# Four small matmuls of a pair of tiles on four quarters of the array instead of two

## The reference, cut to what matters

```python
W = weights[condition]                        # (64, 64, 64), one matrix per sequence
y = jnp.einsum('bct,bcd->bdt', x, W)          # mix over the channels
w = (unpacked - zero_point) * scale           # (1024, 1024), 6-bit values, scale and zero by output row
return x + jnp.einsum('bsk,nk->bsn', y, w) + bias
```

## Time and profile before

| | us |
|---|---|
| median of 3 runs | 293.28 (293.01 to 293.81) |
| the profiled execution's own time | 293.79 |
| its span, first to last instruction | 292.0 |
| TensorE matmuls busy | 285.5 (98%) |
| VectorE busy | 188.3 (65%) |
| GpSimd busy | 91.9 (31%) |
| ScalarE busy | 84.5 (29%) |
| granted TensorE clock | 1.00 of full speed |

### The profile page before, as it was taken

The page is one execution under the profiler, slowest core; times in us unless marked ns, Lnnn a source line. Parts: engine busy times, 40 slices in busy tenths (PEclk is TensorE's granted clock), DMA queues, the critical chain, the costliest instruction groups (busy, mean ns, idle before and its releaser), DMA issues.

```text
span 292.0 us, 8492 instructions
## 1 busy us (share of the span) xinstructions
PE 285.5 (98%) x3299; PEld 234.3 (80%) x3299; DVE 188.3 (65%) x255; ACT 84.5 (29%) x195; POOL 91.9 (31%) x39
## 2 busy tenths in 40 slices
PE   7999999999999999999999999999999999999995
PEld 3867888888888888888888888888888888888884
DVE  3687998655667565566756566675656667565554
ACT  3755334512406050240605023060602306030000
POOL 1019814314143432414343240434324043430000
PEclk9999999999999999999999999999999999999999
DMA  7983646442524344142524415143441510122112
GB/s 248 314 321 96 210 177 200 142 152 77 159 110 135 125 144 151 73 153 108 164 97 144 153 72 189 72 149 112 146 151 72 188 72 36 72 74 74 72 72 73
DMA packets 20547, 39.02 MB, mean 134 GB/s; under 512 B 6835, under 2 KB 7091, under 8 KB 20532
## 3 DMA queue, kind: packets, MB, share of 16 engines
q1 hardware_dynamic: 20100, 37.63, 37.2%
q10 hardware_dynamic: 432, 1.18, 1.1%
HBM read 22.02 MB, written 16.78 MB: 133 GB/s over the span
## 4 chain that ended last, share of the span: by engine, by line
PE 93%; DMA 2%; SPq 2%; ACT 1%; issue 1%; DVE 1%
PE o_ps L301 80%; PE y_ps L259 10%; DMA q_raw<-in_L_ffn_qweight_dram 2%; PE ysum_ps L318 1%; SPq L153 1%; SPq L149 1%; ACT qT L460 1%; PE y_ps L301 1%; DMA ids<-in_itok_B_dram 0%; PE ysum_ps L273 0%; PE qt_ps L283 0%; PE ysum_ps L347 0%; ACT junk L426 0%; SPq L138 0%; DVE q_int L520 0%
## 5 line engine op out<-in xcount | busy, mean ns | idle before, releaser
L301 PE MATMUL o_ps<-qT,y_hi 128*128 128x512 f32 (+1 forms) x520 | 200.6, 389 | 0.4 <-ACT qT L460 0.4
L301 PE MATMUL o_ps<-qT,y_lo 128*128 128x512 f32 (+1 forms) x520 | 198.1, 384 | 0.5 <-issue 0.5
L654 POOL TENSOR_TENSOR resid<-x_sb,bias_bc 128x1024 f32<-128x1024 f32 x32 | 90.8, 2840 | 168.1 <-DVE o_sb L558 149.3
L301 PEld LDWEIGHTS o_ps<-qT,y_hi 128*128 128x128 f32 x520 | 97.2, 188 | 21.9 <-issue 1.5
L301 PEld LDWEIGHTS o_ps<-qT,y_lo 128*128 128x128 f32 x520 | 97.2, 188 | 18.8
L550 DVE TENSOR_TENSOR o_sb<-o_ps,scale_bc 128x512 f32<-128x512 f32 x63 | 43.6, 692 | 82.2 <-PE o_ps L301 82.1
L435 ACT ACTIVATE y_hi<-y_ps 128x512 fp32r<-128x512 f32 x64 | 33.4, 602 | 161.2 <-PE y_ps L259 161.1
L558 DVE TENSOR_TENSOR o_sb<-o_sb,resid 128x512 f32<-128x512 f32 x63 | 52.6, 836 | 2.2
L530 DVE TENSOR_TENSOR y_lo<-y_ps,y_hi 128x512 fp32r<-128x512 f32 x64 | 40.0, 683 | 9.0 <-ACT y_hi L435 9.0
L539 DVE SCALAR_TENSOR_TENSOR resid<-zs_bc,ysum,resid 128x1024 f32<-128x1024 f32 x32 | 43.2, 1350 | 0.0
L259 PE MATMUL y_ps<-w_sb,x_sb 64*64 64x64 f32 x2048 | 35.2, 220 | 0.1
(11 more groups left out here) (33 smaller groups left out, 49.2 us busy)
## 6 DMA issues: line engine op xcount, KB each, us to landing
x_sb<-in_x_dram SPq DMA_DIRECT2D x32, 512.0 KB, 3.5
out_dram<-o_sb SPq DMA_DIRECT2D x63, 256.0 KB, 2.0
q_raw<-in_L_ffn_qweight_dram SPq DMA_DIRECT2D x5, 384.0 KB, 5.8
q_raw<-in_L_ffn_qweight_dram ACTq DMA_DIRECT2D x3, 384.0 KB, 5.1
w_sb<-in_L_cond_weights_dram SPq DMA_DIRECT2D x64, 16.0 KB, 2.0
bias_bc<-in_L_ffn_bias_dram SPq DMA_DIRECT2D x1, 512.0 KB, 8.7
zs_bc<-n_weight_zero_point_dram SPq DMA_DIRECT2D x1, 512.0 KB, 9.4
out_dram<-o_sb SPq DMA_DIRECT2D x2, 128.0 KB, 2.0
```

The costliest lines, as they stand in the source:

```text
L301: last = nc.tensor.matmul(bank, part[:, slot, kt, :], qT[:, kt, col:col + width], start=(kt == 0 and part is y_hi), stop=(kt == KT - 1 and ...
L654: nc.gpsimd.tensor_tensor(resid[:, j % RING, :], x_sb[:, j % RING, :], bias_bc[:], ALU.add).then_inc(xbias_ready, 1)
```

## The change

Only the second tile of a pair (odd `j`) is treated otherwise. Its `half` 0 still reads the upper row half, but writes partitions 64 to 127 of `ysum_ps`; its `half` 1 reads the lower row half and writes partitions 0 to 63 of `qt_ps`. These are the two quarters that the first tile's sums do not use. ScalarE reads the sums from these partitions and writes them to the same partitions of `ysum` as before, so for odd tiles its copy goes from one half of the partitions to the other. The number, the kind and the order of instructions are the same on every engine, and so are the semaphores; no bank of PSUM is used that was not used before.

```diff
                 for half in range(2):
                     rows = slice(half * C, (half + 1) * C)
-                    last = nc.tensor.matmul(ysum_banks[half][rows, slot:slot + 1], w_sb[rows, slot, rows],
+                    place = slice((half + j) % 2 * S, ((half + j) % 2 + 1) * S)
+                    last = nc.tensor.matmul(ysum_banks[half][place, slot:slot + 1], w_sb[rows, slot, rows],
                                             xsum[rows, slot:slot + 1], start=True, stop=True)
                     last.then_inc(ysum_ps_ready, 1)
...
                     act.wait_ge(ysum_ps_ready, t * 2 + half + 1)
-                    last = nc.scalar.activation(ysum[rows, slot:slot + 1], ysum_banks[half][rows, slot:slot + 1],
+                    place = slice((half + j) % 2 * S, ((half + j) % 2 + 1) * S)
+                    last = nc.scalar.activation(ysum[rows, slot:slot + 1], ysum_banks[half][place, slot:slot + 1],
                                                 ACT.Copy, scale=-1.0)
```

## The result

The changed kernel takes 291.63 us in the median of 11 runs (290.94 to 293.34), the kernel before 292.95 us in 11 runs (292.62 to 296.29). The ratio is 0.9942, with a 95% interval of 0.992 to 0.9964: faster by 0.6%, between 1.1 and 2.3 us. The ratio is not that of the two medians, which would be 0.9955 (1.32 us); both lie in the interval. The forecast was 291.9 us.

The account below looks back on a forecast made before the run. TensorE was taken as the bound, its sums-and-mix stage as long as the fullest array quarter. 13 steps x 0.105 us, about 1.4 us, off 293.28 gave 291.9 us; range 291.3 to 292.5, widened to 293.1 for rivals.

Parts of the forecast that it names:

- TensorE alone is the bound, and only the stage of sums and mix changes: Loop step: all 16.98 us are TensorE's; the 14.73 us linear layer stays, the effect lies in the other 2.25 us.
- The fullest quarter sets the stage, 36 loads against 34 at 0.058 us: Sums and mix: two weight loads fewer on each of the two fuller array quarters, 0.116 us less per step.
- The stagger: Head of the sums: third and fourth quarters start 0.01 to 0.02 us later, leaving about 0.10 us gain.
- 0.105 us per step, 1.4 us in all: Sums and mix: net gain per step, ends 0.05 and 0.13 us, taken over 13 steps.
- The median: Whole kernel: 293.28 us, the median of the runs before, less 1.4 us gives 291.9 us.
- Ahead of 52.9 us nothing changes: Start-up before the loop: unchanged, so 0 us in the total.
- The sum: Whole kernel: 1.4 us off gives a span of 290.6 us and a profiled execution of 292.4 us.
- ScalarE's crossing copies cost nothing: ScalarE's four copies per step, two crossing partition halves: 0 us, with some 13 us of cover if dearer.
- Rival A: Sums: second tile's loads start 0.055 us late on a shared row half; gain 0.06 us per step, 292.5 us; chance 0.13.
- Rival B: Sums and mix: four quarters share a load rate already in use; gain 0, 293.3 us; chance 0.12.
- Rival C: Sums: loads wait for matmuls in flight in their row half; 0.14 us more per step, 295.1 us; chance 0.05.

Follow-up runs that it names:

- e9: Changed kernel with each sum issued twice, all four sums once and then all four again: period 16.993 us, ratio to the kernel before 0.9999.
- e3: Changed kernel with only the first tile of a pair summed, its sums copied for the second too: period 16.860 us, ratio to the kernel before 0.9949.
- e2: Kernel before with both tiles' sums on the other two quarters, all four copies crossing partition halves: period 16.980 us, ratio 0.9986.
- e5: Changed kernel with each sum issued twice in direct succession, on four quarters: period 17.013 us, ratio to the kernel before 1.0019.

## Where the prediction was right, and the step that failed

*TensorE alone is the bound, and only the stage of sums and mix changes.* Right: 14.73 us of linear layer in both, 2.25 us against 2.14 for the stage.

*The fullest quarter sets the stage, 36 loads against 34 at 0.058 us.* Right. Fullest quarters of 34, 36 and 40 gave 16.86 to 16.87, 16.98 to 17.01 and 17.23 us. Two loads at the same stagger (changed kernel against e9) are 16.993 - 16.873 = 0.120 us, 0.060 each by the period.

*The stagger takes 0.01 to 0.02 of it.* Right, and now measured: 0.013 us for two more quarters to start (changed kernel against e3; e9 against before).

*0.105 us per step, 1.4 us in all.* The period says 0.107 and 1.39. The two ratios, 0.9942 and 0.9946, stand for 1.7 and 1.6 us; both intervals hold 1.39 us (0.9953).

*The median.* 291.9 was forecast and 291.63 measured. The forecast took 1.4 us off a median of three runs, 293.28; over 11 runs the same kernel has 292.95, and 292.95 - 1.39 = 291.56 is within 0.1 us of what was measured. So the 0.27 us by which the forecast was too high come mostly from its base, which was 0.33 us too high, and not from the gain.

*Ahead of 52.9 us nothing changes.* This is the step that failed. The sum put the start-up at 0 between one execution and another, because its instructions are the same, and no second trace stood behind that. The runs showed -0.68 us there between the two profiled executions (the loop begins at 52.30 us, not 52.98), about half of the 1.39 us that the change brought, and up to 1.3 us between the eleven traces. So the profiled execution took 291.73 us where the sum said 292.4, and the span was 289.9 us where it said 290.6. The 0.68 us is, but for some hundredths, one gap of TensorE in the start-up of the kernel before's first trace; the cause of the gap is open. Read from spans alone, the change would have been credited with half as much again as it did. The mechanism of the gain is untouched by this.

*ScalarE's crossing copies cost nothing.* Right, also with all four crossing (e2).

*Rival A, half the gain because a row half is shared.* Wrong: the third and fourth load start 0.01 to 0.02 us after the first, not 0.055, with two quarters of each row half at work. *Rival B, a shared rate already in use.* Wrong: eight loads more cost 0.013 us (e9 against before) where they fall on the emptier quarters, four fewer gained 0.013 (e3). *Rival C, a load waits for matmuls in its row half.* Wrong: in the changed kernel's step above, the load at 69.12 starts on the upper right 0.02 us after the one on the upper left, whose pass is recorded with 0.21 us (its end is modelled), and the period is 0.107 us shorter, not 0.14 longer as such a wait would have made it; so the rule of the Trainium skill that was cited for it (TensorE: Matmul & The Clock Gate, What overlaps and what doesn't) does not hold in this kernel.

## What to carry to other kernels

Where small matmuls are packed on quarters of the array, count the weight loads on each quarter between two changes of size: in this kernel the stage cost the fullest one, whatever the others did and, but for a stagger of 0.01 to 0.04 us, whatever the order, and a matmul with one column counted as much as one with 64. Two loads moved off each of the two fuller quarters gained what leaving half of the sums out gained, to 0.013 us. For an effect of 0.1 us per step read the period of the loop in the trace, not the span: the part ahead of the loop varied by 1.3 us.

## What the runs showed of the hardware

- Each quarter takes a weight load every 0.055 to 0.058 us (64x64 fp32, granted clock 1.00) independently of the three others, with one column to stream or with 64.
- Work for a free quarter overtakes work for a busy one (0.14 us after the first sum in the earlier trace rows, 0.03 in e2), yet quarters are started in program order, some 0.007 us apart where two loads stand ahead of each next one (0.02 us over three starts in e9) and 0.013 where four do (0.04 in e5). That stagger is not made up over 34 more loads on each quarter: the periods of e5 and e9 differ by the same 0.02 us.
- A copy by ScalarE of 64x1 values from one half of the partitions to the other takes 0.16 to 0.17 us, like one that stays.
